# Splitting the experts' weights inside the softmax attention

## The reference

```python
h = tok_W.T[x] + tok_b + positions                       # embedding
h = h + attention1(layernorm(h))                         # 8 heads of 16, causal, normalised without a softmax
h = h + ffn(layernorm(h))

def ffn(x):
    hx = layernorm(x, ln_g, ln_b)
    q, k, v = heads(hx @ Wq), heads(hx @ Wk), heads(hx @ Wv)      # 2 heads of 64
    q, k = l2norm(q) * 8 * qn_g, l2norm(k) * 8 * kn_g
    o = softmax(where(causal, q @ k.T / 8, min)) @ v
    y = o @ Wo
    gate = softmax(y @ gate_W + gate_b)                           # over 8 experts, all used
    hid = gelu(einsum('bnd,edf->bnef', y, W1) + b1)               # 128 -> 512 in each expert
    eo = einsum('bnef,efd->bned', hid, W2) + b2
    return einsum('bned,bne->bnd', eo, gate)
```

## Time and profile before

| | us |
|---|---|
| median of 3 runs | 964.44 |
| the profiled execution | 964.4 |
| its span, first to last instruction | 962.3 |
| PE busy | 827.2 (86%) |
| DVE busy | 732.0 (76%) |
| ACT busy | 513.4 (53%) |
| POOL busy | 366.6 (38%) |
| mean granted TensorE clock | 0.919 |

### The profile page before, as it was taken

The page is one execution under the profiler, slowest core; times in us unless marked ns, Lnnn a source line. Parts: engine busy times, 40 slices in busy tenths (PEclk is TensorE's granted clock), DMA queues, the critical chain, the costliest instruction groups (busy, mean ns, idle before and its releaser), DMA issues.

```text
span 962.3 us, 21449 instructions
## 1 busy us (share of the span) xinstructions
PE 827.2 (86%) x7864; PEld 592.4 (62%) x7864; DVE 732.0 (76%) x1725; ACT 513.4 (53%) x1069; POOL 366.6 (38%) x478
## 2 busy tenths in 40 slices
PE   1677999999667565888898998699999999999997
PEld 1555777777433333556665666477777777777775
DVE  5736666666579896667667774399999999999997
ACT  1322444444056765667686898455555555555553
POOL 7565555555567774455565676100000000000000
PEclk9887999999656766899999999799999999999999
DMA  3110000000001110000000000000000000000000
GB/s 124 46 26 4 1 0 0 0 0 0 1 22 43 33 41 16 1 1 2 2 2 1 2 2 2 1 2 13 2 12 2 13 3 11 13 2 13 2 13 12
DMA packets 9474, 11.65 MB, mean 12 GB/s; under 512 B 1832, under 2 KB 6704, under 8 KB 9264
## 3 DMA queue, kind: packets, MB, share of 16 engines
q1 hardware_dynamic: 8368, 8.43, 2.9%
q0 software_dynamic: 1024, 2.10, 0.8%
HBM read 8.43 MB, written 2.10 MB: 11 GB/s over the span
## 4 chain that ended last, share of the span: by engine, by line
PE 60%; DVE 11%; POOL 11%; issue 9%; ACT 7%; DMA 0%; DVEq 0%; POOLq 0%; ACTq 0%
PE ps L897 59%; POOL plo L359 3%; DVE mx L794 2%; DVE y L684 2%; ACT phi L520 2%; POOL h_all L221 2%; ACT p L519 1%; POOL rr L306 1%; POOL rr L315 1%; DVE x L726 1%; DVE ss L732 1%; POOL ss L323 1%; ACT ql L506 1%; ACT arena L408 1%; PE ps L1167 0%
## 5 line engine op out<-in xcount | busy, mean ns | idle before, releaser
L897 PE MATMUL ps<-y,arena 128*128 128x512 f16 (+1 forms) x896 | 247.4, 424 | 19.3 <-DVE y L684 17.0
L548 ACT ACTIVATE cst<-ps,col 128x512 f32<-128x512 f32 x256 | 176.1, 688 | 163.6 <-PE ps L897 163.6
L897 PEld LDWEIGHTS ps<-arena,sq 128*128 128x128 f16 x3072 | 192.8, 98 | 60.5 <-DVE sq L883 0.7
L897 PE MATMUL ps<-arena,sq 128*128 128x128 f16 x3072 | 213.0, 219 | 0.5 <-DVE sq L883 0.5
L883 DVE TENSOR_TENSOR sq<-cst,sq 128x512 f16<-128x512 f32 x256 | 175.7, 686 | 4.4
L359 POOL TENSOR_TENSOR plo<-p,phi 128x512 f16<-128x512 f32 (+2 forms) x120 | 124.8, 1058 | 89.8 <-ACT phi L520 88.2
L878 DVE CAST sq<-cst 128x512 f16<-128x512 f32 x256 | 108.0, 422 | 12.2 <-ACT cst L548 3.1
L897 PEld LDWEIGHTS ps<-y,arena 128*128 128x128 f16 (+1 forms) x896 | 75.4, 112 | 58.5 <-issue 24.8
L794 DVE TENSOR_REDUCE mx<-ps 128x1 f32<-128x512 f32 (+3 forms) x160 | 91.3, 604 | 24.6 <-PE ps L897 23.8
L519 ACT ACTIVATE p<-ps 128x512 f32<-128x512 f32 (+3 forms) x160 | 88.2, 552 | 23.8 <-PE ps L897 22.6
L520 ACT ACTIVATE phi<-ps 128x512 f16<-128x512 f32 (+3 forms) x160 | 88.7, 554 | 0.0
(11 more groups left out here) (153 smaller groups left out, 1305.8 us busy)
## 6 DMA issues: line engine op xcount, KB each, us to landing
sq<-w_rows SPq DMA_DIRECT2D x16, 256.0 KB, 2.7
out<-h_all SPq DMA_DIRECT2D x32, 64.0 KB, 1.6
cst<-consts SPq DMA_DIRECT2D x1, 1294.0 KB
h_all<-emb_rows,idx POOLq DMA_INDIRECT x32
wqkv<-w_qkv SPq DMA_DIRECT2D x1, 192.0 KB
wsm<-w_sm SPq DMA_DIRECT2D x1, 192.0 KB
row<-rows SPq DMA_DIRECT2D x1, 140.0 KB
c<-consts SPq DMA_DIRECT2D x1, 96.0 KB
```

The costliest lines, as they stand in the source:

```text
L548: a.activation(hid[:, f], ps[:, HBANK[f], :], ACT.Gelu_apprx_tanh, bias=col[:, K_B1 + k:K_B1 + k + 1], scale=1.0 / WS).then_inc(S["hid_rea ...
L897: return t_.matmul(o, l, r, start=start, stop=stop, skip_group_check=True)
```

## The change

The 16 pieces are no longer split in the projections. In the softmax attention, at steps 6, 14, 22, ... 126 (`WSLOT`), ACT writes the high half of a piece after its exponentials of that step (and after `max_row`, if there is one), and DVE then makes the low half in one operation, stage x 64 - high, straight from the loaded piece. POOL no longer takes part, `scaled` is gone, and SP's loads wait for the low half of the piece before the last. On DVE the new operation stands behind the row maxima and `plo` of its step, and ahead of the head's output and of the stages of the gate.

```diff
-            with sp.Fori(2, NT - 1, 2) as n:
-                for u in range(2):
-                    sp.wait_ge(S["scaled_ready"], n + (u - 1))
-                    sp.dma_start(stage[u], w12_rows[:, ds(n * 512 + u * 512, 512)]).then_inc(S[STAGED[u]], 16)
+            for n in range(2, NPIECE):
+                sp.wait_ge(S["wlow_ready"], n - 1)
+                sp.dma_start(stage[n % 2], w12_rows[:, n * 512:(n + 1) * 512]).then_inc(S[STAGED[n % 2]], 16)
...
-            def weights_low(c, par):
-                pool.wait_ge(S["scaled_ready"], c + 1)
-                piece = w12[:, ds(c * 4, 4), :, :]
-                g.tensor_tensor(piece[:, :, 1, :], scaled[par].rearrange("p (w d) -> p w d", d=D), piece[:, :, 0, :],
-                                ALU.subtract).then_inc(S["split_done"], 1)
...
-            def weights_high(c, par):
-                act.wait_ge(S[STAGED[par]], 8 * (c - par) + 16)
-                act.wait_ge(S["split_done"], c + 1)
-                st = stage[par].rearrange("p (w d) -> p w d", d=D)
-                a.activation(w12[:, ds(c * 4, 4), 0, :], st, ACT.Copy, scale=WS)
-                a.activation(scaled[par], stage[par], ACT.Copy, scale=WS).then_inc(S["scaled_ready"], 1)
+            def weights_high(n):
+                act.wait_ge(S[STAGED[n % 2]], 16 * (n // 2 + 1))
+                a.activation(w12[:, 4 * n:4 * n + 4, 0, :], stage[n % 2].rearrange("p (w d) -> p w d", d=D),
+                             ACT.Copy, scale=WS).then_inc(S["whigh_ready"], 1)
...
                     if k + 2 in FIRST:
                         max_row(FIRST.index(k + 2))
+                    if k in WSLOT:
+                        weights_high(WSLOT.index(k))
...
+            def weights_low(n):
+                piece = w12[:, 4 * n:4 * n + 4]
+                dve.wait_ge(S["whigh_ready"], n + 1)
+                v.scalar_tensor_tensor(piece[:, :, 1, :], stage[n % 2].rearrange("p (w d) -> p w d", d=D), WS,
+                                       piece[:, :, 0, :], ALU.mult, ALU.subtract).then_inc(S["wlow_ready"], 1)
...
                     v.tensor_tensor(plo[:, k % PR, lo:], p32[:, k % QR, lo:], phi[:, k % PR, lo:], ALU.subtract
                                     ).then_inc(S["plo_dve"], 1)
+                if k in WSLOT:
+                    weights_low(WSLOT.index(k))
                 for it in range(len(ITEMS)):
                     if k == OAT[it]:
                         head_out(it)
...
+WSLOT = [8 * n + 6 for n in range(2 * E * FF // 512)]
```

More of the change, by code:

```diff
@@ L151, in tower @@
         stage = [sqf[:, 0:512], sqf[:, 512:1024]]
-        scaled = [sqf[:, 1024:1536], sqf[:, 1536:2048]]
-        oT, y32 = scaled
+        oT, y32 = sqf[:, 1024:1536], sqf[:, 1536:2048]
         hid = cst[:, C_POS:C_POS + 4 * CH].rearrange("p (u t) -> p u t", u=4)
@@ L160, in tower @@
         ps = ctx.enter_context(nc.psum_tensor("ps", [P, 8, 512], F32))
-        names = """load_c load_w load_s load_stage load_stage1 split_done gathered0 gathered1 gathered setup stats veps
+        names = """load_c load_w load_s load_stage load_stage1 whigh_ready wlow_ready gathered0 gathered1 gathered setup stats veps
             rstd hb_ready xn_ready xnT_ps xn0_sb xsT_sb x0_link qkT_ps qkT_sb qkv_ps qkv_sb dt_ps
@@ L167, in tower @@
             vhi_ready vlo_ready qkd_ps hi_ready lo_ready sm_ps sm_used max_link mneg mrow_ps mrow_sb s_ps
-            p_ready plo_pool plo_dve scaled_ready pv_done o_link o_used oT_ps oT_sb y_ps yhi_ready ylo_ready
+            p_ready plo_pool plo_dve pv_done o_link o_used oT_ps oT_sb y_ps yhi_ready ylo_ready
             lg_ps lg_link lg_ready eg_ready gate_ready gT_ps gT_sb b2_ps h2_ready hid_ps hid_ready hhi_ready
@@ L343, in step_a2 @@
                     both_norms(c + 3, 1 - par)
-                weights_low(c, par)
             with pool.Fori(0, NT - 5, 2) as c:
@@ L348, in _ @@
                     step_a2(c + u, u)
-            for c in range(NT - 4, NT):
+            for c in range(NT - 4, NT - 1):
                 step_a2(c, c % 2, NT - 1 - c)
@@ L493, in step_a2 @@
                     normed_T(c + 2, par)
-                weights_high(c, par)
             with act.Fori(0, NT - 5, 2) as c:
@@ L556, in _ @@
             for i, (name, size) in enumerate([("hid_ready", RING), ("w2_done", RING), ("hlo_even", 2), ("hlo_odd", 2),
-                                              ("eo_used", 8), ("qkn_ready", 1), ("lo_ready", 1), ("vlo_ready", 1),
-                                              ("split_done", 2)]):
+                                              ("eo_used", 8), ("qkn_ready", 1), ("lo_ready", 1), ("vlo_ready", 1)]):
                 v.memset(credit[:, i:i + 1], 0.0).then_inc(S[name], size)
@@ L861, in _ @@
             dve.wait_ge(S["lg_link"], 5 * B * NQ)
-            dve.wait_ge(S["split_done"], 2 + NPIECE)
+            dve.wait_ge(S["wlow_ready"], NPIECE)
             def add_rows(n, r):
@@ L1176, in _ @@
                         bank4 = S["h2_ready"], m + 1
-            pe.wait_ge(S["split_done"], 2 + NPIECE)
+            pe.wait_ge(S["wlow_ready"], NPIECE)
             pe.wait_ge(S["ylo_ready"], B * NQ)
```

## The result

The changed kernel takes 977.33 us (median of 4 runs, 972.27 to 980.91). The kernel before has a median of 965.52 in 4 runs, one of which, of 1418.27 us, lies far off; without it the median is 964.44. The ratio leaves that run out: 1.0128 times as long, 95% interval 1.009 to 1.0167, so slower clear of noise, but by under 2%. The profiled execution took 979.05 us, its span 977.1 against 962.3. The forecast was 977 with a range of 960 to 988.

A forecast was written before the change was run, and what follows sets the result against it. It took a loop of waits to pace the projections and TensorE to lead the attention. 964.4 - 5 + 11.5 + 4.5 + 2.5 = 977.9, stated as 977 us, range 960 to 988.

The forecast's parts named there:

- Projections: Second block's projections: removing the split gives back 0.5 us in each of nine steps, -5 us, between 0 and -11.
- The stall: Projections: GpSimd's weight subtraction holds up VectorE's `x` in 13 of 16 steps, mean 0.85 us each.
- the tie at half clock: Projections at 1.2 GHz: two loops equally long, one of them 6.98 us, so removing the stall gives nothing there.
- The loop through rr and `x`: Projections: GpSimd's rr, `x`, VectorE's sum of squares, rr again; 6.02 us without the stall, 7.13 with it.
- the other loop: Projections: hxT, TensorE's projection and transposes, ScalarE's copies, next hxT; 6.98 us at half clock, without slack.
- The wait ahead of the gate: Attention, six gate steps: VectorE's wait for ScalarE's scaling delays the gate product TensorE needs, +11.5 us in sum.
- Long done: Attention, step 22 before the change: the gate product was called long done when TensorE started the transposes at 416.44.
- Plain slots: Attention, the ten slots that are no gate steps: 0.45 us each, +4.5 us, between 0 and 13.
- Clock: Attention: TensorE's clock also falls after steps 30 and 110, 3.4 us at half speed each; +2.5 us (0 to 3.4).
- Rival C: Attention: VectorE's wait is covered, as TensorE waits last for the row copy at four gate steps; 955 us, chance 0.06.
- Rival D: Attention: the fused operation, starting first, holds GpSimd's plo; ten plain slots 0.69 us more, no projections gain; 990, chance 0.06.
- B: Projections' stall comes back in full, plain slots and clock cost nothing: 965 us, range 955 to 974, chance 0.33.

The follow-up runs named there:

- e8: The changed kernel again, unaltered, for a second profile: 978.51 us in one run.
- e4: The changed kernel with all 16 pieces split behind the softmax attention, one after the other: 988.99 us, 1.0277 of the kernel before.
- e3: The changed kernel with its slots at steps 4, 12, 20, ... 124, none a gate step: 979.86 us, 1.019 of the kernel before.
- e7: The kernel before with the fusing alone: split still in the projections, VectorE's fused operation last in its step, no GpSimd subtraction: 961.15 us, 0.9968 of before.
- e1: The changed kernel with VectorE's fused operation moved to the end of its step, ScalarE's scaling left in place: 956.61 us, 0.9963 of the kernel before.
- e5: The changed kernel with the six pieces of the gate steps moved to steps 114, 130, 134, 150, 154 and 158: 961.71 us, 0.999 of before.
- e6: The changed kernel with ScalarE's scaling one step earlier, the fused operation still ahead of the gate: 976.05 us, 1.0122 of the kernel before.
- e11: e6 with GpSimd's low halves cut to 16 columns at the six gate steps and the two steps ahead of each: 958.4 us in one run.
- e10: e1 once more, for a second profile: 957.47 us, 0.9975 of the kernel before.

## Why the prediction was right

- **Projections**, forecast -5: measured -8.7 in the profile shown, -7.1 in e8, -6.7 in e4, -2.7 in e3, all against the one profile of before. The stall, its cause and its end are as forecast (e7, and the rows of `x`), and so is the tie at half clock: 6.98 became 6.85. The gain hangs on the clock, as forecast: e3, with 105.7 of 122.8 us at 1.2 GHz, gained least; in the other ten profiles with the same projections as the changed kernel they took 116.4 to 118.8 us. Undersized was the step at full clock, forecast to fall towards 6.1 and measured at 5.37. The loop through rr and `x` runs ahead during the slow steps, where the other loop binds (from `x` to its `hxT` 2.4 us at 282.3 and 3.7 at 301.6), and lets the fast ones go below its own length. I gave back 0.5 us a step with the loops side by side, as if each step were bound by the longer one.
- **The wait ahead of the gate**, forecast +11.5 by single steps of 2.1, 2.3 (three), 1.3 and 1.15: measured +10.1, by +2.0, +2.1 (three), +1.0 and +0.9. This was the main term, its mechanism stands in the timeline, and e1 and e5 take it away in two independent ways. "Long done" was too much said of the gate product of step 22 before (0.65 us in hand, 0.16 at step 46), which only made a delay there the surer to be felt. Of GpSimd's hold, 0.27 us forecast for steps 30, 46 and 110, the fused operation felt 0.07 to 0.09. e6 and e11 showed what the forecast had not asked: taking ScalarE's wait away alone gives back only 3.0 of the 10.1, since the collision with GpSimd is waiting behind it, and the scaling put earlier delays ScalarE's row copy.
- **Plain slots**, forecast +4.5: what is left of TensorE's added idle time is 12.9 - 10.1 = 2.8 us, a remainder and not a measurement of the ten slots. In e5, with 16 slots of this kind, the attention is 3.5 us longer.
- **Clock**, forecast +2.5: the same 2447 matmuls are busy for 6.9 us longer. The two further falls came where forecast, at steps 30 and 110, but each lasted 6.8 us and not 3.4, and those at steps 22 and 62 doubled too. This is the term that was mis-sized: the forecast took 3.4 us for the length of every fall, and 1.7 us each as the most it could cost. That the long waits bring the low clock is supported by the two going together: 40.1, 39.7, 39.9 and 36.6 us of it in the changed kernel, e8, e3 and e6, and 12 to 25 in all the others. It is not a simple measure of the waits: e11, with 11.2 us of gate waits, has 12.8 us of low clock, and the kernel before, with 7.9, has 24.2. What made e1, e10 and e11 stay at 12 to 13 us stays open.
- That 977 meets the median of 977.33 so closely is luck; the errors compensate: -5 + 11.5 + 4.5 + 2.5 = 13.5 against -8.7 + 10.1 + 2.8 + 6.9 = 11.1, to which the unchanged first stage and the other two stretches added 3.9 us of their own in this profile.
- **Rival C** (covered wait) is refuted by the releaser at all six slots. **Rival D** has the mechanism right and the size wrong: where VectorE's operation starts first, GpSimd's does take longer (in e6 1.44 us behind the fused operation of 576.26, in e3 1.22 to 1.24 beside twelve of the slots, against 1.155), but GpSimd's busy time in the attention is 133.92 us against 132.01 with the same 127 operations, 2 us in all and not 7. **B**, at 965, would have needed the stall back in full, plain slots for nothing and the clock to stay up; they were 8.7 of 11, 2.8 and 6.9.

The version with the change's gain and without its loss is e1: twice measured, 0.9963 and 0.9975 of the kernel before, both intervals below 1, if barely (0.9993 and 0.9999). By moving two lines it is some 16 us faster than the changed kernel (by the ratios, 1.0128 against 0.9963), but only 3.3 and 2.3 us faster than the kernel before; the two profiled executions differ by 9.1 us, since that of the kernel before is one of its longer ones.

## What to carry to other kernels

When work is moved into an engine's holes, ask in each slot what stands behind it on that engine and who is waiting for that, before adding up busy times: 0.7 us of VectorE's work, with 0.63 of ScalarE's ahead of it, made TensorE wait 0.9 to 2.1 us longer in each of six slots and about 0.3 in each of ten, before the slower clock is counted. Put a filler last in its step, behind every short chain that the leading engine needs, and look at more than one such chain (e3 traded the gate for the row maxima). If its input is late and it also collides with a neighbour's work, removing one of the two delays may only uncover the other; and an input made earlier delays what stands behind it on the engine that makes it (e11).

## What the runs showed of the hardware

- An operation of VectorE with two SBUF inputs that started during one of GpSimd's subtractions `plo` did not end before it, however small: the gate product of 32 columns took 0.19 us alone, 0.43 to 0.80 at five of the six gates of the kernel before, and 0.99 in e6; the fused operation took 0.69 and 1.37. Where VectorE's started first, GpSimd's took longer: 1.44 us in e6 from 576.52, with the fused operation from 576.26 to 576.94, against a median of 1.155. The Trainium skill (SBUF — State Buffer, section on the two separate sides) says that whichever of two such operations starts first has the shared port pair for its whole length, and these runs agree. Beside `x`, GpSimd's subtractions in the projections kept to 1.151 to 1.159 us.
- VectorE's fused scale and subtraction of 128x512, f32 and f16 in, f16 out, took 0.691 us at its shortest in the changed kernel, the same as most of the plain subtractions `plo` of this shape (0.691 to 0.693): the scaling is free in it.
- At steps 22, 30, 62 and 110 of the changed kernel TensorE's granted clock fell to 0.50 inside waits of 2.8 to 3.5 us, after 3.4 us in which TensorE was busy for 1.17 to 1.95, and stayed there for 6.8 us though TensorE had work again (busy for 5.27 of 6.80 at step 22). Behind the waits of 2.9 and 2.8 us at steps 46 and 86 it stayed for 3.4. The 10.1 us of added gate waits thus came with 6.9 us of slower matmuls.
